# One register load per bucket in two graph layers, and one wide product in two expert mixtures

## The reference, cut to what matters

```python
def _rgcn_layer(x, W, self_w, b, src, dst, edge_type, num_nodes):      # 8 relations
    xW = jnp.einsum('ni,rio->rno', x, W)
    msg = xW[edge_type, src]
    agg = jax.ops.segment_sum(msg, dst, num_segments=num_nodes)
    return agg + x @ self_w + b

# mixture of 8 experts, the best 2 per node; hidden width 1024 (relu; exact gelu in the second mixture)
h = relu(x @ W1[e].T + b1[e])
y = h @ W2[e].T + b2[e]
out = out + combine[..., e:e + 1] * y

x = x + L0_gnn(layernorm(x))      # two relational layers
x = x + L0_ffn(layernorm(x))      # first mixture
x = x + L1_gnn(layernorm(x))      # three degree-normalised layers over the same edges, and a projection
x = x + L1_ffn(layernorm(x))      # second mixture
```

## Time and profile before

| | |
|---|---|
| median of three runs | 2473.8 us (2470.71 to 2475.99) |
| the profiled execution's own time | 2470.25 us |
| its span, first to last instruction | 2468.5 us |
| PE busy | 1972.6 us, 80% of the span |
| DVE busy | 1393.6 us, 56% |
| ACT busy | 867.1 us, 35% |
| POOL busy | 893.5 us, 36% |
| mean granted TensorE clock | 0.897 of full speed |

### The profile page before, as it was taken

The page is one execution under the profiler, slowest core; times in us unless marked ns, Lnnn a source line. Parts: engine busy times, 40 slices in busy tenths (PEclk is TensorE's granted clock), DMA queues, the critical chain, the costliest instruction groups (busy, mean ns, idle before and its releaser), DMA issues. The chain is left out here.

```text
span 2468.5 us, 42256 instructions
## 1 busy us (share of the span) xinstructions
PE 1972.6 (80%) x11984; PEld 1670.6 (68%) x11984; DVE 1393.6 (56%) x3174; ACT 867.1 (35%) x2015; POOL 893.5 (36%) x859
## 2 busy tenths in 40 slices
PE   3777777778677777777848999967989884899987
PEld 2566566656455555556737999956878774799986
DVE  4555555555355555555544555546545566566664
ACT  4333333332333333333301333324545441233332
POOL 3775555551475444455301433322000000233432
PEclk9889998998898888889967999988999995799998
DMA  6566656554565555555656354234767649424261
GB/s 211 184 210 191 192 182 201 188 188 132 188 201 187 172 174 170 185 177 182 220 216 262 89 153 118 40 70 144 250 209 249 227 141 363 141 40 118 42 189 28
DMA packets 190071, 420.94 MB, mean 171 GB/s; under 512 B 25476, under 2 KB 101232, under 8 KB 185712
## 3 DMA queue, kind: packets, MB, share of 16 engines
q1 hardware_dynamic: 139144, 308.52, 35.4%
q0 software_dynamic: 48096, 106.74, 17.6%
q10 hardware_dynamic: 2568, 2.56, 0.3%
HBM read 256.77 MB, written 113.77 MB: 150 GB/s over the span
## 5 line engine op out<-in xcount | busy, mean ns | idle before, releaser
L2209 PE MATMUL ps<-ring,halves 128*128 x3384 | 581.8, 327 | 17.0 <-SPq L2171 9.4
L2209 PEld LDWEIGHTS ps<-ring,halves 128*128 128x128 f32 x3384 | 486.1, 192 | 61.6 <-issue 18.7
L1387 PE MATMUL ps<-slots,rows 128*128 128x128 f32 x2504 | 427.5, 300 | 71.2 <-issue 35.3
L1387 PEld LDWEIGHTS ps<-slots,rows 128*128 128x128 f32 x2504 | 394.9, 213 | 125.7 <-issue 59.5
L1416 PE MATMUL ps<-fixed,sums 128*128 128x256 f32 x1280 | 388.8, 419 | 55.6 <-DVE sums L1298 54.3
L1130 POOL DMA_INDIRECT rows<-tab_h,gidx_node x313 | 311.2, 994 | 319.9 <-PE ps L1387 169.9
L1293 DVE TENSOR_TENSOR sums<-sums,ps 128x256 f32 x626 | 263.1, 420 | 259.4 <-PE ps L1387 127.8
L1130 POOL DMA_INDIRECT rows<-tab_x,gidx_node x313 | 313.1, 1000 | 248.2 <-PE ps L1387 139.2
L1334 DVE TENSOR_SCALAR scratch<-fixed,scratch,count_key 128x640 f16<-128x640 f16 x480 | 219.5, 457 | 205.2 <-issue 173.7
L1436 PE MATMUL ps<-scratch,fixed 128*128 128x320 f16 x960 | 217.7, 326 | 147.3 <-DVE scratch L1334 144.5
L1416 PEld LDWEIGHTS ps<-fixed,sums 128*128 128x128 f32 x1280 | 234.2, 210 | 79.6 <-DVE sums L1298 61.8
(11 more groups left out here) (245 smaller groups left out, 2135.1 us busy)
## 6 DMA issues: line engine op xcount, KB each, us to landing
ring<-split_weights SPq DMA_DIRECT2D x16, 4096.0 KB, 14.9
sums<-fixed SPq DMA_DIRECT2D x80, 576.0 KB, 4.9
split_weights<-fixed SPq DMA_DIRECT2D x176, 256.0 KB, 2.4
slots<-tab_counts SPq DMA_DIRECT2D x40, 640.0 KB, 4.1
fixed<-in_ffn_units SPq DMA_DIRECT2D x88, 256.0 KB, 4.0
split_weights<-weight_pieces SPq DMA_DIRECT2D x80, 256.0 KB, 2.5
tab_counts<-fixed SPq DMA_DIRECT2D x20, 640.0 KB, 4.6
strip<-tab_counts SPq DMA_DIRECT2D x20, 640.0 KB, 4.2
```

Source lines behind the costliest of these rows:

```text
L1387: last = t_.matmul(psS[t % len(psS)][:, k * P:(k + 1) * P], rows[:, s * D + k * P:s * D + (k + 1) * P], self.onehots[:, h * P:(h + 1) * P] ...
L2209: ins = nc.tensor.matmul(to, lhs[left], weights(slot, right, at, n), start=first and (left, right) == (0, 0), stop=last and left == 1)
```

## The change

In the relational layers `at` is loaded in the bucket's first step only and kept in its register for the six pair one-hots. In the mixtures the high half of the activations meets both halves of the weights in one product of 512 columns, whose two result halves lie side by side in the PSUM bank; low by high still goes to the first half. `take_y` adds the second half in an instruction of its own, with a semaphore between the two.

```diff
                     i, late = divmod(t, SPACING)
                     if i < len(buckets):
-                        at = dve.value_load(self.window[0:1, buckets[i]:buckets[i] + 1], min_val=0, max_val=ETILES - WINDOW)
                         if late:
                             count_hots(i, at, late - 1)
                         else:
+                            at = dve.value_load(self.window[0:1, buckets[i]:buckets[i] + 1], min_val=0, max_val=ETILES - WINDOW)
                             source_hots(i, at)
...
+            def both_halves(slot, at, n):
+
+                by_half = self.big[:, :].rearrange("p (h w) -> p h w", h=2)
+                return by_half[:, :, bass.ds(slot * WE + at, n)].bitcast(F32R)
...
-                        last = products(psY[i % 2][:, 0:D], [x[:, c * P:(c + 1) * P] for x in (hT_high, hT_low)], slot,
-                                        W1E + c * D, D, c == 0, c == HC - 1)
+                        at = W1E + c * D
+                        if c:
+                            nc.tensor.matmul(psY[i % 2][:, 0:D], hT_low[:, c * P:(c + 1) * P], weights(slot, 0, at, D), start=False, stop=False)
+                        last = nc.tensor.matmul(psY[i % 2][:, 0:2 * D], hT_high[:, c * P:(c + 1) * P], both_halves(slot, at, D),
+                                                start=(c == 0), stop=(c == HC - 1))
+                        if c == 0:
+                            nc.tensor.matmul(psY[i % 2][:, 0:D], hT_low[:, c * P:(c + 1) * P], weights(slot, 0, at, D), start=False, stop=False)
                     last.then_inc(y_full, 1)
...
-                    nc.vector.tensor_tensor(ysum[s], psY[s][:, 0:D], bias(e, H, D), ALU.add).then_inc(y_summed, 1)
+                    nc.vector.tensor_tensor(ysum[s], psY[s][:, 0:D], bias(e, H, D), ALU.add).then_inc(y_step, 1)
+                    dve.wait_ge(y_step, i + 1)
+                    nc.vector.tensor_tensor(ysum[s], ysum[s], psY[s][:, D:2 * D], ALU.add).then_inc(y_summed, 1)
```

More of the change, by code:

```diff
@@ L2148, in experts @@
                 "x_turned", "x_step", "xT_ready", "h_full", "h_ready", "h_turned", "g_ready", "hT_ready", "y_full", "y_summed", "y_ready")
-            expert_ready, refilled = sem("expert_ready", "refilled")
+            expert_ready, refilled, y_step = sem("expert_ready", "refilled", "y_step")
             x_steps = 3 if affine else 1
```

## The result

| | before | after |
|---|---|---|
| median | 2474.33 us (2470.71 to 2475.99) | 2188.88 us (2186.49 to 2191.19) |
| profiled execution, its span | 2470.25, 2468.5 us | 2186.49, 2184.8 us |
| mean granted clock | 0.897 | 0.922 |
| layer 1, first to last add | 572.5 us, pitch 1.835 | 425.1 us, pitch 1.363 |
| layer 2 with counts | 507.4 us, pitch 2.02 | 376.9 us, pitch 1.50 |

The change is faster: 0.8848 of the time before, 95% interval 0.8833 to 0.8863. It is the time of the rival "DVE stays the bound", 2189, which had a chance of 0.13. The spans differ by 283.7 us: 147.4 from layer 1, 130.5 from the counted part of layer 2, 3.4 from each mixture; the rest takes back 1.0.

The account below looks back on a forecast made before the run. No engine was full; engines waiting for each other, with DVE's sequencer late through register loads, set the pace. From 2470.25 us, 219 for the loads and 4.5 for the mixtures gave 2247, stated as 2250; range 2185 to 2335.

Parts of the forecast that it names:

- DVE stays the bound: Rival, relational layers: DVE's need falls by 0.50 in both, gain 280 us, time 2189; chance 0.13.
- The step with a pair one-hot: Relational layers: without the register load, add to add takes 0.97 us instead of 1.60.
- DVE's need: DVE's own time per step, relational layers: from 1.69 to 1.19 us in layer 1, 1.87 to 1.37 in layer 2.
- What is late next: Relational layers: PE takes over half of the gap; needs 1.30 and 1.38 us, new pitches 1.49 and 1.57.
- the excess of 0.19: Pitch above the busiest engine's need in layer 2's last 61 steps, in us, taken for both layers after the change.
- the old excess of 0.14 and 0.15: Pitch above DVE's need before the change, in us a step, in layer 1 and in layer 2's counted steps.
- The 1.30 for PE: Layer 1: mean of the longer engine's need, PE's 1.335 us in 12 of 15.65 steps, DVE's 1.19 otherwise.
- 1.24: POOL's gathers: their pitch in us when they needn't wait, below the new 1.49 of the steps.
- the gathers become late: Rival, relational layers: each gather waits for two DVE one-hots, 0.90 us more, kernel 126 us slower, about 2595; chance 0.02.
- The wide product: Mixtures, `down`: a chunk takes 0.352 instead of 0.360 us, 6.0 us gained over 94 tiles.
- the 1.5 us at the ends: Mixtures: cost of the second addition in `take_y`, showing only at three places, 0.5 us each.
- Half clock: Rival, relational layers: granted clock stays 0.90 and 0.87 with PE the longer engine; gain 150 us, time 2319.

Follow-up runs that it names:

- e7: The changed kernel with the bucket's register load put back in three of its six pair one-hot steps (240 of the 480 removed loads): 2325.18 us.
- e6: The changed kernel with five of the 18 multiply products of each node tile left out, so PE has less work: 2184.98 us.
- e10: The changed kernel with the place of each add a number known at build time and every fourth gather left out once the ring is full: 2099.61 us.
- e5: The changed kernel with the place of each add put in as a number at build time, removing the register loads before the adds: 2127.10 us.
- e9: The changed kernel with the places of four adds loaded by one instruction every fourth step, whole output computed: 2154.32 us.
- e12: e5 with the low piece cut to one column and, from the third bucket on, the source one-hots cut to one element: 2089.29 us.

## Why it came out below the forecast

The time lies inside the range because the range had been drawn to take in most of what the rival "DVE stays the bound" would give, and only 4 us from its lower end; the forecast's own sum missed it.

**The step with a pair one-hot: right.** 0.97 us was predicted and read. "Issue" before the one-hots is gone, PE's wait before counts is a twelfth of what it was.

**DVE's need: right in its change.** It was to fall by 0.50 a step in both layers, and the pitches fell by 0.47 and 0.52. e7 shows the same in halves. That the rival's time was met to the microsecond is luck: the two layers miss its 0.50 in opposite directions, and in layer 1 POOL stands beside DVE.

**"What is late next": the step that failed.** It let PE take over half of the gap, and took the excess of 0.19 from the last steps of layer 2 as what two engines of equal need lose. Both fell. e6 took work from PE and nothing changed; e7 gave the second half of the gain in full. DVE stayed the bound: its need of 1.19 and 1.37 with the old excess of 0.14 and 0.15 would give 1.33 and 1.52, and 1.363 and 1.502 were measured, with POOL's gathers at 1.333 close behind in layer 1. The 1.30 for PE was too high: e10 runs at 1.223 in all. That sum took the longer engine step by step, PE in steps with a multiply and DVE in the others, as if each step had to end before the next. By the prediction's own prices PE's work alone is 0.45 + 0.24 + 12 x 0.645 / 15.65 = 1.185 a step, and e10 shows 1.223. And the last steps aren't held by two engines alike: e5 touched DVE's loads alone and took 9.2 us from those 78.6, 0.15 a step, while e6 took work from PE and left 78.0. So most of that 0.19 hung on the load of `add`, not on a play of two engines. The two errors together cost (1.49 - 1.363) x 308 + (1.57 - 1.502) x 252 = 56 us, nearly all of the 61.

**What the excess of 0.14 in the counted steps is made of** stays open. e9 takes 0.05 of the pitch away with three of four loads, so part of it may be DVE's sequencer too. Another part may lie in DVE's waits for PE's `aggregate` before the adds, 121.8 us after and still 112.0 in e6, where PE has less to do. That the two engines are tied together by four PSUM banks is an untested rival: no run gave them more.

**POOL: sized too low.** 1.24 came from two gathers that nothing held up; the mean pitch is 1.333, level with DVE in layer 1. The rival "the gathers become late" had its mechanism right in part, a DVE instruction that holds a gather up, and its instruction and size wrong: not the pair one-hots, and 0.09 a gather rather than 0.90. Most of that was there before the change: layer 1's mean gather was 1000 ns before and 1028 after. The Trainium skill says, on the page "SBUF — State Buffer" (section "Who interferes with whom"), that a DVE instruction with two SBUF inputs contends with a GpSimd instruction that reads SBUF. The gather reads its row numbers (`gidx_node`) from SBUF, and e12 agrees, by 1029 against 962 ns. The sign that was named for it, POOL no longer waiting for PE, did come: 309.0 us before, 38.8 after.

**The wide product: right in its price.** `down` takes 2.82 us, the chunk 0.3525; the mixtures gave 6.8 us by their rows; the 1.5 us at the ends are not to be seen. By the rule of the Trainium skill (page "TensorE: Matmul & The Clock Gate", section "Wait — 56ns, not 53.3ns?"), with 2.5 ns for each product saved, it would have been 1.9, an estimate; the rows of this kernel, 6.8 us or 9 ns for each product saved, don't agree.

**Half clock: did not come.** The granted clock rose, and PE was not the bound.

## What to carry to other kernels

An engine that looks 56% busy, as DVE did here, can be the bound through its sequencer: count the register loads in its loop as work, and read the distance between instructions, not their busy time. When an engine is relieved, work out the next bound engine by engine over a whole period; the longer one of each step, added up, overstated it here (1.30, where e10 ran at 1.223). And a stretch that serves as the measure of "what two engines lose" must first be shown to be held by both.

## What the runs showed of the hardware

Instructions of DVE overlap: 0.34 us from the start of an add to the one-hot's and 0.35 from a one-hot's to the piece's behind it, where they last 0.42 and 0.44. One load that fills four registers, in place of four loads, is worth 34.6 us here (e9). A gather that takes 0.94 us undisturbed was up to 1.7 us long beside the source one-hots, a DVE instruction with two SBUF operands (the maximum in e5 is 1727 ns).
